# Cross-attention scores accumulated from key differences, and a step's 64-row matmuls gathered ahead of both products

## What is computed

```python
# B=4, S=1024, D=512, H=8, HD=64; x (4,1024,512), ctx (4,1024,1024), mask (4,1024)
kv = ctx @ W_src.T + b_src                # keys and values, times mask
q  = layernorm(x) @ W_tgt.T + b_tgt       # times mask
scores = einsum('bthd,bshd->bhts', q, k) / 8      # -inf where mask == 0
attn = softmax(scores)
x = x + tanh(g) * (concat(layernorm(x), attn @ v) @ W_out.T + b_out)
x = x + tanh(g2) * ffn(layernorm(x))      # two bit-linear layers, a conv of 3 taps, silu
```

## Time and profile before

| what | value |
|---|---|
| median of 3 runs | 1748.87 us |
| the profiled execution | 1751.08 us |
| its span | 1749.3 us |
| granted TensorE clock, mean | 0.981 |
| PE busy | 1644.8 us (94%) |
| DVE busy | 1137.5 us (65%) |
| ACT busy | 836.4 us (48%) |
| POOL busy | 724.3 us (41%) |
| DMA queues, share of 16 engines | 32.9% |

### The profile page before, as it was taken

One profiled execution on the slowest core, in us unless ns is written; L12 is line 12 of the kernel. 1 busy time (PEld: TensorE's weight loads), 2 busy tenths in 40 slices (PEclk: granted clock), 3 DMA queues, 4 the chain that ended last, 5 costly groups with the idle time before them and its releaser, 6 DMA issues. The chain is left out here.

```text
span 1749.3 us, 23957 instructions
## 1 busy us (share of the span) xinstructions
PE 1644.8 (94%) x8754; PEld 1009.1 (58%) x8754; DVE 1137.5 (65%) x2183; ACT 836.4 (48%) x901; POOL 724.3 (41%) x314
## 2 busy tenths in 40 slices
PE   6999999999998999999999999999999878797978
PEld 5788788888885544455444544454446444454544
DVE  7787634444436667656876677657734977969493
ACT  3233312222210344434564355524565988879776
POOL 1231000000000488856786577756871624426160
PEclk9999999999999999999999999999999989899989
DMA  7787555444434411113132133202143211020302
GB/s 258 267 278 247 195 182 184 164 165 163 161 144 151 152 62 62 65 69 110 62 110 97 57 114 110 86 2 109 54 156 119 71 55 37 23 75 1 97 0 79
DMA packets 109480, 200.88 MB, mean 115 GB/s; under 512 B 9280, under 2 KB 34880, under 8 KB 109376
## 3 DMA queue, kind: packets, MB, share of 16 engines
q1 hardware_dynamic: 109376, 199.50, 32.9%
HBM read 124.75 MB, written 74.71 MB: 114 GB/s over the span
## 5 line engine op out<-in xcount | busy, mean ns | idle before, releaser
L791 POOL TENSOR_TENSOR acc<-acc,pr 128x1024 f32<-128x1024 f32 x188 | 448.7, 2387 | 130.5 <-ACT pr L821 113.9
L821 ACT ACTIVATE pr<-ps,mcol 128x1024 f32<-128x1024 f32 x256 | 284.5, 1115 | 362.9 <-PE ps L1591 357.7
L1110 DVE CUSTOM_DVE_ANT_0 junk<-ps,mbias 128x512 bf16<-128x512 f32 x512 | 333.1, 689 | 129.8 <-PE ps L1566 125.4
L1603 PE MATMUL ps<-pr,vv 128*64 128x512 f32 x1024 | 273.8, 616 | 0.0
L798 POOL TENSOR_TENSOR h_first<-h_first,last_tap 128x1023 f32<-128x1023 f32 x43 | 105.3, 2451 | 177.0 <-DVE h_first L1443 146.4
L772 POOL MEMSET nmt<- 128x128 f32 x1 | 0.2, 205 | 343.4 <-DVE chl L1344 343.4
L1566 PE MATMUL ps<-kh,qh 64*128 64x512 f32 x512 | 123.1, 452 | 11.0 <-DVE nmv L1110 9.8
L791 POOL TENSOR_TENSOR acc<-pr 128x1024 f32<-128x1024 f32 x32 | 76.9, 2402 | 122.5 <-ACT pr L821 122.5
L1566 PEld LDWEIGHTS ps<-kh,qh 64*128 64x128 f32 x512 | 50.9, 184 | 128.7 <-issue 99.4
L1848 PE MATMUL ps<-w2q,hq 128*128 128x512 bf16 x512 | 123.0, 395 | 1.5 <-ACT hq L1002 0.7
L1691 PE MATMUL ps<-xiT,w1q 128*128 128x512 bf16 x512 | 121.2, 380 | 2.7 <-DVE x2t L1472 2.7
(11 more groups left out here) (175 smaller groups left out, 3147.1 us busy)
## 6 DMA issues: line engine op xcount, KB each, us to landing
craw<-in_ctxT SPq DMA_DIRECT2D x8, 2048.0 KB, 8.9
xa<-in_x SPq DMA_DIRECT2D x32, 256.0 KB, 3.9
wraw<-in_w1T SPq DMA_DIRECT2D x16, 512.0 KB, 5.9
wraw<-in_w2T SPq DMA_DIRECT2D x16, 512.0 KB, 6.6
q_split<-kqh SPq DMA_DIRECT2D x32, 256.0 KB, 2.1
q_split<-kql SPq DMA_DIRECT2D x32, 256.0 KB, 2.4
base<-lna SPq DMA_DIRECT2D x32, 256.0 KB, 3.7
k_split<-kqh SPq DMA_DIRECT2D x32, 256.0 KB, 2.0
```

The costliest lines, as they stand in the source:

```text
L791: nc.gpsimd.tensor_tensor(acc[:, blk % 2, :], first, pr[:, (8 * blk + j) % NP, :], ALU.add).then_inc(pool_acc, 1)
L821: act.activation(pr[:, u % NP, :], ps[:, 2 * (u % 2):2 * (u % 2) + 2, :].rearrange("p a t -> p (a t)"), ACT.Exp, bias=mcol[:, (u // 64) * ...
L1110: dve.tensor_tensor_reduce(out=(junk1 if n < LEAD and n % 2 else junk)[:, e, :], in0=ps[:, first_bank(n) + e, :], in1=mbias[:, b % 2, kk * ...
L1603: last = pe.matmul(ps[64 * e:64 * e + 64, 6 + blk % 2, :], vv[g % 2][:, j, 64 * e:64 * e + 64], pr[:, u % NP, e * CH:(e + 1) * CH], start= ...
```

## The change

- **Key differences.** Stage B also makes, for each key tile `j` of 2 or more, keys of tile `j` minus keys of tile `j-2`. Its fp32r part goes to DRAM as a third plane of `kd` (from the new `kdh`), and `kql` now holds the low part of the difference (tiles 0 and 1 keep their own keys). `carry` keeps the last 256 keys of a half for the next. `kqh` (whole keys) is still stored, for the tops.
- **Scores of tiles 2 to 7** are added to what tile `j-2` left in the same banks: three terms with the differences, and no `aug1`·`maug` term, since the maximum is in the bank already.
- **Order of a step**: tops, both scores, tops, then both products, with `pe_rows`, `sums` and `project` between the two products.
- **Places and loads**: `acc` moves to the region of `w2q`, whose load now waits for the last sum; `kd_hi` takes the former place of `vv0`; `vv0` takes that of `acc`, so `load_vv(0)` goes behind the last chunk. `load_qk(1)` goes into the last chunk, behind its key stores, and each `load_lo` has a third 512 KB load.

```diff
-    kd = nc.dram_tensor("k_split", (B * PAIRS, 2, P, S), F32).ap()
+    kd = nc.dram_tensor("k_split", (B * PAIRS, 3, P, S), F32).ap()
...
             def load_lo(g):
                 sp.dma_start(ql[g % 2][:].bitcast(F32), qd[g, 1]).then_inc(sp_lo[g % 2], 16)
                 sp.dma_start(kl[g % 2][:].bitcast(F32), kd[g, 1]).then_inc(sp_lo[g % 2], 16)
+                sp.dma_start(kd_hi[g % 2][:].bitcast(F32), kd[g, 2]).then_inc(sp_lo[g % 2], 16)
...
-                    for w, t in ((0, kqh), (1, kql)):
+                    for w, t in ((0, kqh), (1, kql), (2, kdh)):
...
+            sp.wait_ge(pe_z, 2 * NG)
             sp.dma_start(w2q[:], w2q_d.rearrange("(k p) o -> p k o", p=P)).then_inc(sp_w2, 16)
...
                     act.activation(kqh[:, m % 2, :], kq[:, m % 2, :], ACT.Copy).then_inc(act_b, 1)
+                    act.wait_ge(dve_b, c * B_DVE_N + B_DVE[f"db{m}"])
+                    act.activation(kdh[:, m % 2, :], kql[:, m % 2, :].bitcast(F32), ACT.Copy).then_inc(act_b, 1)
+                    act.activation(carry[:, m, :], kq[:, m % 2, 2 * P:CH], ACT.Copy).then_inc(act_b, 1)
...
+            def key_steps(dn, an, m, half):
+                diff, keys = kql[:, m % 2, :].bitcast(F32), kq[:, m % 2, :]
+                dve.wait_ge(act_b, an + B_ACT[f"kh{m}"])
+                dve.wait_ge(dve_b, dn + B_DVE[f"k{m}"])
+                if half:
+                    dve.tensor_tensor(diff[:, 0:2 * P], keys[:, 0:2 * P], carry[:, m, :], ALU.subtract).then_inc(dve_b, 1)
+                else:
+                    dve.tensor_copy(diff[:, 0:2 * P], keys[:, 0:2 * P]).then_inc(dve_b, 1)
+                dve.tensor_tensor(diff[:, 2 * P:CH], keys[:, 2 * P:CH], keys[:, 0:2 * P], ALU.subtract).then_inc(dve_b, 1)
+
+            def key_low(dn, an, m):
+                dve.wait_ge(act_b, an + B_ACT[f"dh{m}"])
+                dve.wait_ge(dve_b, dn + B_DVE[f"db{m}"])
+                dve.tensor_tensor(kql[:, m % 2, :], kql[:, m % 2, :].bitcast(F32), kdh[:, m % 2, :].bitcast(F32), ALU.subtract).then_inc(dve_b, 1)
...
-                terms = ((kh[g % 3][:, keys], qh[g % 3][:, tokens]), (kl[g % 2][:, keys], qh[g % 3][:, tokens]),
-                         (kh[g % 3][:, keys], ql[g % 2][:, tokens]), (aug1[:], maug[g % 2][:, tokens]))
+                terms = ((kd_hi[g % 2][:, keys], qh[g % 3][:, tokens]), (kl[g % 2][:, keys], qh[g % 3][:, tokens]),
+                         (kd_hi[g % 2][:, keys], ql[g % 2][:, tokens]), (aug1[:], maug[g % 2][:, tokens]))
+                if j >= 2:
+                    terms = terms[0:3]
...
-                                         start=w == 0, stop=w == 3)
+                                         start=j < 2 and w == 0, stop=w == len(terms) - 1, skip_group_check=True)
...
-            for s in range(MACROS):
-                for a in range(2):
-                    if 2 * s + a < UNITS:
-                        score(2 * s + a)
-                    if s == 0 and a == 0:
-                        pe.wait_ge(dve_b, NCH * B_DVE_N)
-                    if a == 0 and 2 * s + LEAD < UNITS:
-                        pe_tops(pe, 2 * s + LEAD)
-                for a in range(2):
-                    if 0 <= 2 * s - 2 + a < UNITS:
-                        product(2 * s - 2 + a)
-                    if a == 0 and 2 * s + LEAD + 1 < UNITS:
-                        pe_tops(pe, 2 * s + LEAD + 1)
+            def between_products(s):
                 if s in TURNS:
                     pe_rows(pe, TURNS[s])
-                if s in ZBLK:
+                if s in ZBLK and ZBLK[s] < LAST:
                     sums(ZBLK[s])
...
+            for s in range(MACROS):
+                if 2 * s + LEAD < UNITS:
+                    pe_tops(pe, 2 * s + LEAD)
+                for a in range(2):
+                    if 0 < 2 * s + a < UNITS:
+                        score(2 * s + a)
+                if 2 * s + LEAD + 1 < UNITS:
+                    pe_tops(pe, 2 * s + LEAD + 1)
+                for a in range(2):
+                    if 0 <= 2 * s - 2 + a < UNITS:
+                        product(2 * s - 2 + a)
+                    if a == 0:
+                        between_products(s)
```

More of the change, by code:

```diff
@@ L133, in flamingo_gated_block @@
         maskc = sb("maskc", [P, NCH * CT], F32)
+        kdh = sb("kdh", [P, 2, CH], F32R)
+        carry = sb("carry", [P, PAIRS, 2 * P], F32)
         assert used["at"] <= CRAW
@@ L160, in flamingo_gated_block @@
         used["at"] = TOP_AB
-        vv, ql, kl, maug = [], [], [], []
+        kd_hi, vv, ql, kl, maug = [], [], [], [], []
         for i in range(2):
-            vv.append(sb(f"vv{i}", [P, NT, P], F32))
+            if i == 0:
+                kd_hi.append(sb("kd_hi0", [P, S], F32R))
+            else:
+                vv.append(sb("vv1", [P, NT, P], F32))
             ql.append(sb(f"ql{i}", [P, S], F32R))
@@ L197, in flamingo_gated_block @@
         xic = sb("xic", [P, NT, D], BF16)
+        acc = sb("acc", [P, 2, 2 * CH], F32)
+        assert used["at"] <= TOP_W
         used["at"] = XN + 4 * NT * D + 8 * S
@@ L344, in flamingo_gated_block @@
         n = 0
-        for name in ([f"{w}{m}" for m in range(PAIRS) for w in ("k", "kl")]
+        for name in ([f"{w}{m}" for m in range(PAIRS) for w in ("k", "da", "db", "kl")]
                      + [w + str(j // 2 if w[0] == "w" else j) for j in range(CT)
@@ L350, in flamingo_gated_block @@
         B_DVE_N = n
-        B_ACT = {name: i + 1 for i, name in enumerate([f"kh{m}" for m in range(PAIRS)]
+        B_ACT = {name: i + 1 for i, name in enumerate([f"{w}{m}" for m in range(PAIRS) for w in ("kh", "dh", "cy")]
                                                       + [f"vh{j}" for j in range(CT)])}
@@ L642, in b_chunk @@
                     load_maskb(b + half, 1 - half)
+                if last and half:
+                    for sl in range(2):
+                        sp.wait_ge(sp_k_out[sl], 48 + 96 * NCH)
+                    sp.wait_ge(act_b, c * B_ACT_N + B_ACT[f"cy{PAIRS - 1}"])
+                    load_qk(1)
                 for j in range(CT):
@@ L678, in _ @@
             load_mrow(0)
-            load_qk(1)
             sp.dma_start(mcol[:], mask_cols).then_inc(sp_mcol, 16)
             load_lo(0)
-            for sl in range(2):
-                sp.wait_ge(sp_v_out[sl], 16 + 32 * (NCH - 1))
-            load_vv(0)
             b_chunk(B - 1, 1, True)
             for sl in range(2):
-                sp.wait_ge(sp_k_out[sl], 32 + 64 * NCH)
+                sp.wait_ge(sp_k_out[sl], 48 + 96 * NCH)
                 sp.wait_ge(sp_v_out[sl], 16 + 32 * NCH)
@@ L690, in _ @@
             sp.wait_ge(pe_bv, NCH * CT + 8)
+            load_vv(0)
             sp.wait_ge(dve_b, NCH * B_DVE_N)
@@ L1355, in b_chunk @@
                         dve.wait_ge(dve_b, dn + B_DVE[f"kl{m - 2}"])
+                        dve.wait_ge(act_b, an + B_ACT[f"cy{m - 2}"])
                     dve.scalar_tensor_tensor(out=kq[:, m % 2, :], in0=ps[:, m, :], scalar=bk[:, m:m + 1], in1=maskb[:],
                                              op0=ALU.add, op1=ALU.mult).then_inc(dve_b, 1)
-                    dve.wait_ge(act_b, an + B_ACT[f"kh{m}"])
-                    dve.wait_ge(dve_b, dn + B_DVE[f"k{m}"])
-                    dve.tensor_tensor(kql[:, m % 2, :], kq[:, m % 2, :], kqh[:, m % 2, :].bitcast(F32), ALU.subtract).then_inc(dve_b, 1)
+                    key_steps(dn, an, m, half)
+                    key_low(dn, an, m)
                 for j in range(CT):
@@ L1651, in c_pe @@
                         project(b, i)
+            score(0)
+            pe.wait_ge(dve_b, NCH * B_DVE_N)
+            for s in range(MACROS):
[11 more added lines that the diff above has]
+                        between_products(s)
+                if s in ZBLK and ZBLK[s] == LAST:
+                    sums(LAST)
             ln_row(pe, 0)
```

20 lines of the change are left out of this document (11 added, 9 removed).

## The result

The changed kernel takes 1721.93 us (median of 4 runs, 1721.26 to 1724.19), the kernel before 1749.47 us beside it (4 runs, 1747.53 to 1750.27): a ratio of 0.9846, 95% interval 0.9829 to 0.9864. The profiled execution took 1721.26 us, span 1719.5. The gain is 27.5 us by the medians (29.8 by the profiled executions) where 35.8 were forecast.

The account below looks back on a forecast made before the run. PE's own instruction stream was taken to bound stages B and C. Terms of 83.4 us less and 47.6 more took 35.8 from the profiled 1751.1, giving 1715.3, and 1713 us after a 2.2 us run correction; range 1686 to 1738.

Parts of the forecast that it names:

- Dropped term, 0.46 per light step: Stage C steps on key tiles 2 to 7 lose two matmul pairs: 40.0 us less, plus 2 in the tail.
- Grouping, 0.34: Stage C: two fewer changes between 64-row and 128-row work save 0.34 us per step, 39.4 us less over 116 steps.
- A new wait, 0.29: Light steps of stage C: second tops wait for DVE's 1.90 us read loop, 0.29 us each, 25.2 us back.
- POOL and DVE, 6.9 us: Stage C: POOL's add holds `lower` on DVE, 0.3 us in each of 23 blocks without projections, 6.9 us back.
- The signs: Trace and page: light steps about 4.2 us, POOL's idle before adds under half, `lower` mean well above 1 us.
- Stage B at nothing, start 2 us: Stage B's added work costs nothing; at the start `mcol` right behind `mbias` gives 2 us less (0 to 2.1).
- Layer norms, 8 us: Two stage C steps per batch: strings of small DVE instructions delay tops, 8 us back (0 to 11).
- between the products, 3.8: Stage C: `pe_rows` and `project` get one more change of shape, 0.1 us each in 38 places, 3.8 us back.
- `load_vv`, 0.8: Start of stage C: `load_vv(0)` lands a good 1 us after the first product's former start, 0.8 us back.
- Rival 1: Stage C: second tops do not hold PE and DVE is not locked out; 63.3 us less, 1686 us; chance 0.22.
- Rival 2: Stage C: `lower` waits for a whole add in every block, 43.7 us instead of 6.9; about 1750 us; chance 0.06.
- Rival 3: Stage C: POOL becomes the bound with stretched adds; 13 us more, 1762 us; chance 0.04.

Follow-up runs that it names:

- group_psum: Kernel before with the new step order alone, no key differences, `upper` ahead of its step's first exponential and `un` kept in its PSUM bank: 1713.39 us.
- half_tops: The changed kernel with DVE reading 256 of the 512 columns of each bank of tops, half of the maxima left out: 1690.61 us.
- no_dve_wait: The changed kernel with the edits of half_tops and upper_short together: 1650.15 us.
- psum_un: upper_first with the normalised product `un` written back to its PSUM bank, so `lower` reads PSUM and SBUF; whole computation kept: 1699.61 us.
- upper_short: The changed kernel with `upper` ahead of its step's first exponential and POOL's adds on 512 of 1024 columns, half of the sums left out: 1690.17 us.
- before_psum: Kernel before with `un` kept in its PSUM bank and read there by `lower`, `upper` not moved: 1744.31 us.
- upper_first: The changed kernel with ACT's `upper` ahead of its step's first exponential instead of behind it: 1716.02 us.
- lower_late: The changed kernel with DVE's `lower` behind the second tops of its step instead of behind the first: 1719.93 us.

## Why the prediction was right, and where it was not

Direction and range held (1721.9 in 1686 to 1738); the forecast of 1713 was 9 us too low.

- *Dropped term, 0.46 per light step*: right. In the tail a light step takes 3.45 us where the earlier trace rows have 3.91. The tail was priced too low: its blocks fell from 16.53 to 15.13 us, 1.40 where three light steps make 1.38, so about 4 us and not 2. POOL did not bind, but only just: its adds ended at 1267.42, 0.36 us ahead of the sums that need them.
- *Grouping, 0.34*: right (group_psum, 1.3 per block with the 0.1 for `sums`).
- *A new wait, 0.29*: right to the hundredth (4.20 in the change, 3.91 in half_tops and no_dve_wait).
- *POOL and DVE, 6.9 us* is the step that failed. The loss at `lower` is at least 22.3 us in the change (psum_un), of which 6.7 were there before: 15.6 new, against 6.9. I asked when the lock would meet `lower` and took it that DVE could start `lower` at about 1.9 us into the block. It started at 662.06 - 658.91 = 3.15 us, because of a second wait in the same place: `uh` on ACT, behind an exponential whose scores the new order puts behind the tops. Rows of before did not show it (7.4 us in 4 places), but the order of both engines did. By these numbers the gain is 15.6 - 6.9 = 8.7 us less than forecast, with 2 more in the tail: 35.8 - 8.7 + 2 = 29.1 against 29.8 by the profiled executions. So near an agreement is partly luck. Priced by upper_short, where shorter adds hold `mbias` less as well, the loss is 31.8 and not 22.3 us, and three other terms, 12.6 us together, were never measured singly. What holds without that choice: my sum without this term is 35.8 + 6.9 = 42.7 us, and from before_psum to psum_un it was 43.1.
- *The signs*: two of them failed. `lower` has a mean of 982 ns where "well above 1 us" was foretold, 984 before; POOL's idle time fell by a tenth where more than half was. Both fit the cause above: DVE stood still instead of being locked, and longer blocks left POOL its gap. Its seven adds (15.00 / 6 = 2.50 apart) take 17.5 us, 0.1 less than I took, but blocks of 18.7 and 19.8 are longer than that.
- *Projection blocks*: I let them gain as the others. They fell by 0.1 to 0.7 us, where in psum_un it is 1.1 to 1.6: six of PE's waits in `project` were for `ul`, 11.3 us.
- *Stage B at nothing, start 2 us*: right within 1 us each (stage B 0.7 longer; `mcol` 1.4 earlier, the first product, at 591.45, 0.7 earlier). A slip on the way: 24 x 0.23 is 5.5 us and not 5.4, and nothing hangs on it. *Layer norms, 8 us; between the products, 3.8; `load_vv`, 0.8*: not measured singly.
- *Rival 1* (no wait for tops, no lock; 1686) did not happen. The kernel made to have neither, no_dve_wait, took 1650, 36 us below it: the price of the wait, 25.2 us, was near (half_tops, 31.3), but no_dve_wait also takes away the 6.7 us that before had lost at `lower`, and its longest blocks fell by 3.2 us. The rest is not split. *Rival 2* (lock at full price, 1.9 us) did not happen in the change; in upper_first it was 1785 - 690 = 1.1 us in the mean, and 2.65 - 0.69 = 1.96 in the longest. *Rival 3* did not happen: adds stayed at 2389 ns in the mean, 2.50 apart.

## What to carry to other kernels

When an edit moves an instruction earlier on one engine, read what stands behind it on the engine that consumes it: anything there that waits for a third engine now waits longer, and everything queued behind it comes late. Two losses on one engine can hide each other, so test their removal together as well as singly. Where DVE and POOL both work on SBUF, one operand left in PSUM took DVE's instruction out of the conflict in all 32 blocks; look then at what meets the adds in its place (here `mbias`). And when a total does not move, compare it by block before calling an edit worthless.

## What the runs showed of the hardware that I had not expected

PE's granted clock fell to its lower level after PE had been held in stage C. lower_late, busy time by stretch (us; PE, PEld, DVE, ACT, POOL, clock):

```profile
675.00:680.00 5.00, 5.00 (x36) 2.86 (x34) 3.98 (x12) 2.63 (x3) 4.65 (x3) 1.00 0.00 0
680.00:685.00 5.00, 2.78 (x12) 1.15 (x12) 4.08 (x6) 2.12 (x2) 4.71 (x3) 0.86 0.00 0
685.00:690.00 5.00, 5.00 (x15) 1.64 (x13) 1.92 (x7) 0.00 (x0) 1.93 (x1) 0.50 0.02 5
```

and PE's timeline there:

```profile
683.02 1.40 PE L1596 MATMUL ps<-kh,qh 64*128 64x512 f32 x2 [2.10 <-DVE nmv L1125]
684.35 1.97 PE L1635 MATMUL ps<-pr,vv 128*64 128x512 f32 x4
686.25 0.48 PE L1603 MATMUL ps<-ident,nmt 128*128 128x128 f32 x1
```

A product takes 686.25 - 684.35 = 1.90 us where it takes 0.95 at full clock: 0.50 is 1.2 GHz, against 2.4. From the product at 684.35 to the next step's second tops at 691.12 it took 6.77 us, where the same rows in half_tops take 4.00 at full clock (719.46 to 723.46). So behind a wait of 2.1 us the slow stretch cost 2.8 us more; PE had stood still just before. In the change the same was seen twice: 0.50 from 588 to 590 us behind a wait of 0.79 us, and 0.56 from 874.0 to 877.4 behind one of 1.07 us. From 600 to 1300 us before had one such place, psum_un and lower_late three, upper_short and no_dve_wait none. It does not follow each wait. In half_tops the clock stayed at 1.00 behind this one:

```profile
717.17 0.75 PE L1596 MATMUL ps<-kh,qh 64*128 64x512 f32 x2 [1.33 <-DVE nmv L1125]
```

What decides is not settled by these runs, nor is how much of lower_late's loss is clock and how much lock; no kernel parted them.

An instruction with a single SBUF input, `mbias`, was long beside an add as well: 2.65 us in psum_un and 2.87 in lower_late, against 1.36 in the change and 0.69 at 531.30 in the change, where POOL stood idle.
